# Issuing each 128-column one-hot matmul of the last scatter-sum as four 32-column ones

## The reference, cut to what matters

```python
msg = h[edge_src]
agg = jax.ops.segment_sum(msg, edge_dst, num_segments=h.shape[0])
mean = agg * deg_inv[:, None]
return h @ W_self + mean @ W_neigh + b
```

## Time and profile before

| what | us |
|---|---|
| two timed executions | 3285.64 and 3287.21 |
| their median | 3286.43 |
| the profiled execution, first to last instruction | 3292.1 |
| of it, the stage of the last aggregation (its first to its last sum matmul and the last add) | 2306 to 2993 |

### The profile page before, as it was taken

One profiled execution on the slowest core, in us unless ns is written; L12 is line 12 of the kernel. 1 busy time (PEld: TensorE's weight loads), 2 busy tenths in 40 slices (PEclk: granted clock), 3 DMA queues, 4 the chain that ended last, 5 costly groups with the idle time before them and its releaser, 6 DMA issues. The chain is left out here.

```text
span 3292.1 us, 61715 instructions
## 1 busy us (share of the span) xinstructions
PE 2940.5 (89%) x19999; PEld 1682.0 (51%) x19999; DVE 2208.3 (67%) x3758; ACT 1221.8 (37%) x2818; POOL 1517.3 (46%) x1504
## 2 busy tenths in 40 slices
PE   5577998699999985999799999996899999998999
PEld 4344555388888873444244444443344444443444
DVE  8786878688888897888466666664455555555333
ACT  3564554598888883444122222222000000001111
POOL 2002232367777772222566666661565656552000
PEclk6688999899999998999899999998999999999999
DMA  2896996489999986776799999994999999996454
GB/s 80 273 294 212 330 311 204 157 303 363 348 361 349 352 300 202 219 219 210 293 338 350 343 353 350 363 360 165 358 340 321 340 333 339 324 355 233 137 142 126
DMA packets 271674, 934.22 MB, mean 284 GB/s; under 512 B 43263, under 2 KB 44267, under 8 KB 271375
## 3 DMA queue, kind: packets, MB, share of 16 engines
q0 software_dynamic: 206144, 709.74, 60.4%
q1 hardware_dynamic: 65230, 220.77, 21.4%
HBM read 838.14 MB, written 130.54 MB: 294 GB/s over the span
## 5 line engine op out<-in xcount | busy, mean ns | idle before, releaser
L1743 PE MATMUL gagg_sum_ps<-gagg_got,gagg_hot_hi 128*128 128x256 f16 x3320 | 575.8, 274 | 59.7 <-DVE sums_acc L1691 26.3
L1778 POOL DMA_INDIRECT agg_got<-h_rows,all_run_idx x415 | 412.6, 994 | 336.1 <-PE agg_sum_ps L1839 195.0
L1646 POOL DMA_INDIRECT gagg_got<-xs_rows,all_set_idx x415 | 460.3, 1109 | 169.4 <-issue 85.0
L1709 ACT ACTIVATE gagg_hot_hi<-gagg_hot,all_mem 128x128 f16<-128x128 f16 x1660 | 507.0, 387 | 81.3 <-DVE gagg_hot L1664 80.2
L2130 POOL DMA_INDIRECT agg_got<-h_rows,all_run_idx x415 | 420.8, 1014 | 251.1 <-PE agg_sum_ps L2286 139.7
L1811 DVE TENSOR_TENSOR sums_acc<-agg_sum_ps,sums_acc 125x1024 f32 x220 | 269.2, 1224 | 293.9 <-PE agg_sum_ps L1839 292.3
L1743 PE MATMUL gagg_sum_ps<-gagg_got,gagg_hot_lo 128*128 128x256 f16 x1660 | 454.8, 274 | 0.0
L1839 PE MATMUL agg_sum_ps<-agg_got,agg_hot 128*128 128x512 f16 x1660 | 400.3, 383 | 50.5 <-DMA agg_got<-h_rows,all_run_idx 40.4
L2195 DVE TENSOR_TENSOR sums_acc<-agg_sum_ps,sums_acc 125x1024 f32 x220 | 269.0, 1223 | 232.1 <-PE agg_sum_ps L2286 231.0
L2286 PE MATMUL agg_sum_ps<-agg_got,all_mem 128*128 128x512 f16 x1660 | 391.9, 382 | 22.4 <-DMA agg_got<-h_rows,all_run_idx 19.3
L1743 PEld LDWEIGHTS gagg_sum_ps<-gagg_got,gagg_hot_hi 128*128 128x128 f16 x3320 | 286.8, 97 | 111.3 <-DVE sums_acc L1691 38.0
(11 more groups left out here) (370 smaller groups left out, 4152.9 us busy)
## 6 DMA issues: line engine op xcount, KB each, us to landing
gatw_piece<-slot_rows POOLq DMA_DIRECT2D x52, 512.0 KB, 9.8
split_w<-edg_w_out SPq DMA_DIRECT2D x32, 512.0 KB, 7.7
agg_got<-h_rows,all_run_idx POOLq DMA_INDIRECT x830, 8.4
x_rows<-fin_val POOLq DMA_DIRECT2D x25, 500.0 KB
h_rows<-fin_h POOLq DMA_DIRECT2D x25, 500.0 KB
out_dram<-neigh_rows POOLq DMA_DIRECT2D x24, 500.0 KB, 3.6
norm_x_sb<-in_x_dram SPq DMA_DIRECT2D x25, 448.0 KB
fin_x_sb<-in_x_dram SPq DMA_DIRECT2D x25, 448.0 KB
```

Source lines behind the costliest of these rows:

```text
L1646: g.indirect_dma_start(out=got[:, u % R, :], out_offset=None, in_=rows_in[:, :], in_offset=bass.IndirectOffsetOnAxis(ap=set_idx[:, col:col ...
L1709: last = a.activation(hot_hi[:, u % HOTS, h, :], hot[:, u % HOTS, :], ACT.Copy, scale=high_e[:, ds(begins[g] + j, 1), h])
L1743: last = t.matmul(sum_ps[g % 2][:, h * C:(h + 1) * C], hot_k[:, u % HOTS, h, :], got[:, u % R, part * D + h * C:part * D + (h + 1) * C], s ...
L1778: g.indirect_dma_start(out=got[:, k % R, :], out_offset=None, in_=rows_in[:, :], in_offset=bass.IndirectOffsetOnAxis(ap=run_idx[:, col:col ...
```

## The change

Each of the four matmuls of a chunk becomes four matmuls, one for each 32 columns of `hot`. A matmul with 32 stationary columns writes 32 partitions, so the four write partitions 0 to 31, 32 to 63, 64 to 95 and 96 to 127 of the same columns of `sum_ps`. All four read the same moving columns. Each has its own weight load. The order of the chunks, the semaphores and everything else stay as they are; `mm_done` is raised by the last of a chunk's 16 matmuls where it was by the last of four.

```diff
                             for part in range(2):
                                 for q in range(2):
                                     over = slice(part * D + q * HALF, part * D + (q + 1) * HALF)
-                                    last = t.matmul(sum_ps[g % 2][:, q * HALF:(q + 1) * HALF], hot[:, u % R, :], got[:, u % R, over],
-                                                    start=(u == at[g] and part == 0), stop=(u == at[g + 1] - 1 and part == 1))
+                                    for strip in range(0, P, P // 4):
+                                        last = t.matmul(sum_ps[g % 2][strip:strip + P // 4, q * HALF:(q + 1) * HALF],
+                                                        hot[:, u % R, strip:strip + P // 4], got[:, u % R, over],
+                                                        start=(u == at[g] and part == 0), stop=(u == at[g + 1] - 1 and part == 1))
                             last.then_inc(mm_done, 1)
```

## The result

The changed kernel takes 3326.8 us (median of two, 3325.3 and 3328.3) where the kernel before takes 3286.4: a ratio of 1.0116, 95% interval 1.0087 to 1.0146. It is slower by 40 us, within the 2% that counts as no change; 3334 was predicted. Six more executions of the same kernel, timed on another occasion beside the kernel before, gave 1.0085 (1.0068 to 1.0101), 28 us. The difference between the two figures is taken up with the first two experiments.

The account below looks back on a forecast made before the run. PE was taken to set the pace in the stage's middle part, DMA close behind. Terms 0 + 42 + 13 - 7 = +48 us on the median 3286.4 gave 3334 us, 8-in-10 range 3282 to 3385.

Parts of the forecast that it names:

- Strips side by side, 0 us: Sum matmuls, middle part of the stage: four strips overlap within one matmul's 0.216 us, adding 0 (bounds 0 and 977 us).
- Changes of shape, 42 us: Middle part, TensorE: 350 changes between 128-column and 32-column work, 0.12 us each, range 0 to 0.163.
- The near row: Earlier trace: two matmuls on 4 rows, then 128-row ones; the wide one began 0.07 us before its predecessor's end.
- The lag of the fourth strip, 13 us: Before each of 175 changes from strips to wide work, the fourth strip's later start adds 0.075 us.
- Waits given back, -7 us: Middle part: half of PE's 14.6 us of waits for fetched rows disappears, ends 0 and -14.6.
- Loads, instructions, ends at nothing: Added weight loads hidden, 9960 more instructions fetched without delay, and the stage's first and last parts unchanged: no cost.
- the full drain with an exposed load: Rival: each change of shape costs 0.26 us, +97 us in all, 3383 us; chance 0.20.
- Strips one after another: Rival: the array takes one moving stream at a time; about 4345 us, 32% slower; chance 0.14.
- loads that don't hide: Rival: strips overlap but their weight loads are exposed, a round takes 0.392 us; +300, 3586 us; chance 0.06.

Follow-up runs that it names:

- the first two experiments: e1 and e2: the kernel before and the changed kernel, each run again without edits; ratios 0.9993 and 1.0085 against the kernel before.
- e8: Changed kernel, but after a group's first round all four strips write partitions 0 to 31; measured 4072 us, 781 over the kernel before.
- e3: Changed kernel with the product's matmuls also issued as four 32-column strips, leaving 50 changes of shape; ratio 1.0016 to the kernel before, +5 us.
- e1: The kernel before, run again without an edit as a control; ratio 0.9993, -2 us.
- e2: The changed kernel, run again without an edit; ratio 1.0085 to the kernel before, +28 us.
- e9: Changed kernel with strips for the high parts only, whole matmuls for the low parts, 754 changes of shape; ratio 1.0197 to the kernel before, +65 us.
- e7: Kernel before with each 512-column sum matmul issued as four of 128 moving columns, no change of shape; ratio 1.0024, +8 us.
- e5: Kernel before, whole matmuls, with the product in three pieces of 16 matmuls in place of six of 8; ratio 1.0105, +35 us.
- e4: Changed kernel with each sum matmul as two of 64 columns in place of four of 32; ratio 1.0094 to the kernel before, +31 us.

## Why the prediction was right

**Strips side by side, 0 us.** Right. Rounds stay at 0.216 us, and e8 shows that this rests on the four places. The prediction took 0 as a judgement, and no row before showed it; the reason that it gave, that the strips share neither columns nor output partitions, is what e8 takes away. The Trainium skill ("TensorE: Matmul & The Clock Gate", "Part 3: Packing small matmuls") says that matmuls in different column groups run concurrently, and the trace agrees: four last 0.40 us where one lasts 0.38. The same part of the Trainium skill says that loads overlap running matmuls only on different row groups; here the measurement differs: the strips lie on the same rows, and their loads hide (e3: 1.73 us, as before).

**Changes of shape, 42 us.** The mechanism and the count of 350 are right; the size was 0.12 us and is 0.10 to 0.11 with everything that hangs on a change. The near row's own reading was better than the value that I took: transferred from the earlier trace rows, a successor begins 0.07 before the end of its predecessor, which gave 0.09; the changed kernel shows 0.07 too. That row was one example, of another kind (4 rows changing to 128, not 32 columns), so that it fits as closely as this was in part luck. The rest, 0.01, is the strips' lag and a first matmul that lasts 0.01 longer. With 350 x 0.105 = 37 us this term holds the lag as well, for which 13 us stood apart.

**The lag of the fourth strip, 13 us.** Mis-sized: 0.075 us was expected, from narrow matmuls that follow each other in the same columns, and the strips start within 0.01 us. The lag is 2 us at most, and is in the 37. The 4 ns of the Trainium skill's "Part 3: Packing small matmuls" were nearer than the 25 taken.

**Waits given back, -7 us.** Right: 13.6 to 5.7 us in e1 and e2, -8. In e9, with more changes, nearly all of the wait is swallowed (1.3 us is left).

**Loads, instructions, ends at nothing.** Right for loads and instructions, by e7 (+8 us for as many matmuls, all of which 56 ns distances can account for: 1508 x 0.006 = 9) and e3. The ends are nearly right: the last part of the stage is 1 to 2 us longer. The rate of 24 instructions in a us, at which the cover was called thin, did no harm: e3 takes 36.

**The sum.** 37 - 8 = 29 us, where e2 gave 28, against 48 predicted. The middle parts of e1 and e2 say the same without the count: PE's busy time grew by 34.6 us (612.10 to 646.74, 0.099 for each of 350 changes), and the rest of the part shrank by 8.6. Most of the 20 us too many are the lag (13 for 2) and the 0.12 (42 for 35 without the lag). That the first comparison's 40 us is nearer to the prediction is luck: it rests on two executions, and none of the prediction's terms accounts for it. Of the rivals, the full drain with an exposed load (0.26 us) fell: a change costs 0.10 to 0.11, and the load adds 0.01 of it. Strips one after another and loads that don't hide (rounds of 0.864 and 0.392 us) fell with the rounds of 0.216. The Trainium skill's "TensorEngine Tiling (Array Packing)", section "Key Properties", says "Changing tiling mode (not just tile) drains the TensorE"; the trace agrees in that every change of shape costs and that going from place to place in a round costs nothing to be seen (four starts within 0.01 us), and the wait ends 0.07 us ahead of the modelled end.

What stays open: why the first profile began the stage some 6 to 12 us later than the other runs without a change ahead of it (it was late long before: L1487 first starts at 566.8 us there, and at 557.1 to 564.9 in the eleven others, with 558.7 in e2, the same kernel); why PE's clock was lower in e5; and whether more buffers would have spared e5 its waits.

## What to carry to other kernels

Splitting a matmul's stationary columns into 32-column ones in four places cost nothing here as long as TensorE stayed in that shape (e3); into 64-column ones it cost nothing within a run of sums (e4). Count how often the order alternates between shapes, price each change at 0.1 us, and subtract the waits that it only fills. Where a trace holds a single example of the thing to be priced, take its reading and don't split the difference with a guess. A small gain or loss is not placed by two executions and one profile: compare the stage itself over repeated profiles, and its granted clock with it (e5).

## What the runs showed of the hardware

Four 32-column matmuls on the same moving columns start within 0.01 us of each other and take the 0.216 us of one (changed kernel, e3); in one place they take 0.216 each (e8). A change between 128 and 32 (or 64) columns costs 0.09 us of waiting, in both directions and for 512-column matmuls as for transposes (changed kernel, e4); the successor begins 0.07 us before the modelled end of its predecessor, and the first matmul after it takes 0.01 longer, 0.02 with the 110 ns loads of 64 columns.
